# Two attention layers on one TensorE queue: key tiles weighed in pairs behind the former group's sums, the transposed maxima 65 wide, all positions moved

## The reference, cut to what matters

```python
# layer 0: 32 heads of 32; layer 1: 16 heads of 64
dots = einsum('bhnd,bhmd->bhnm', q, k) * scale
attn = softmax(dots, axis=-1)
out = einsum('bhnm,bhmd->bhnd', attn, v) @ w_out + b_out
```

## Time and profile before

| what | us |
|---|---|
| median of 3 runs (lowest to highest) | 3464.93 (3464.24 to 3469.18) |
| the profiled execution, its own time | 3465.76 |
| span of its trace | 3464.0 |
| layer 0, first to last `rows` product (63 groups) | 288.7 to 1479.2 |
| layer 1, the same | 2084.7 to 3199.0 |
| TensorE busy over the span | 3034.1 (88%) |
| DVE, ACT, POOL busy | 2162.0, 1718.8, 1746.4 |

### The profile page before, as it was taken

How to read it: one execution, slowest core, us unless ns; L and a number is a source line. 1 busy time by engine, 2 the same in 40 slices (tenths; PEclk the granted TensorE clock), 3 DMA queues, 4 the chain that set the end, 5 groups by cost and what they waited for, 6 DMA issues and landing times. The chain is left out here.

```text
span 3464.0 us, 46558 instructions
## 1 busy us (share of the span) xinstructions
PE 3034.1 (88%) x16106; PEld 1908.5 (55%) x16106; DVE 2162.0 (62%) x4520; ACT 1718.8 (50%) x3306; POOL 1746.4 (50%) x1540
## 2 busy tenths in 40 slices
PE   7999999999999999988863839999999999999266
PEld 6884455454545555467752835555555555554166
DVE  5567766676676666646665416676666666666642
ACT  5555766666666666656540414444443444443032
POOL 0005878788787878830101824443444445445056
PEclk9999999999999999989985969999999999999578
DMA  2003333333333333300010444443434444433034
GB/s 88 1 19 89 86 85 91 76 82 85 84 85 89 84 84 75 75 25 16 13 41 25 84 95 92 92 98 82 104 86 92 98 95 95 96 86 70 25 69 74
DMA packets 182987, 254.00 MB, mean 73 GB/s; under 512 B 35904, under 2 KB 75584, under 8 KB 182208
## 3 DMA queue, kind: packets, MB, share of 16 engines
q1 hardware_dynamic: 168672, 240.19, 29.4%
q0 software_dynamic: 14080, 10.82, 2.3%
HBM read 33.44 MB, written 16.67 MB: 14 GB/s over the span
## 5 line engine op out<-in xcount | busy, mean ns | idle before, releaser
L1737 POOL TENSOR_TENSOR arena<-arena 128x512 f32<-128x512 f32 x1152 | 1440.7, 1277 | 859.2 <-ACT arena L1119 835.6
L780 PE MATMUL psum<-stack 96*128 96x512 f32 (+4 forms) x4096 | 1330.2, 442 | 60.3 <-DMA stack<-halves 43.4
L1375 DVE TENSOR_REDUCE top<-psum 128x1 f32<-128x512 f32 x1536 | 1001.0, 685 | 401.4 <-PE psum L780 397.4
L1119 ACT ACTIVATE arena<-psum 128x512 f32<-128x512 f32 x1536 | 857.9, 595 | 448.6 <-PE psum L780 441.4
L780 PEld LDWEIGHTS psum<-stack 96*128 96x128 f32 (+4 forms) x4096 | 712.4, 191 | 639.5 <-issue 399.1
L810 PE MATMUL psum<-arena,values 128*32 128x512 f32 (+1 forms) x3072 | 556.5, 617 | 0.1
L1706 POOL TENSOR_SCALAR rstd<-mv 128x4 f32<-128x4 f32 x56 | 12.6, 226 | 579.2 <-DVE mv L1241 577.5
L768 PE MATMUL psum<-xT,wqkv 128*128 128x512 f32 x512 | 268.6, 606 | 6.8 <-DVE arena L1420 3.0
L1407 DVE RECIPROCAL psum<-psum 128x128 f32<-128x128 f32 x256 | 226.4, 926 | 61.0 <-PE psum L840 61.0
L1082 ACT ACTIVATE halves<-psum,bqk 128x512 fp32r<-128x512 f32 x128 | 87.9, 687 | 310.3 <-PE psum L768 310.2
L1327 DVE SCALAR_TENSOR_TENSOR X<-psum,weight,X 128x128 f32<-128x128 f32 x512 | 144.0, 345 | 141.3 <-PE psum L747 141.2
(11 more groups left out here) (154 smaller groups left out, 3054.5 us busy)
## 6 DMA issues: line engine op xcount, KB each, us to landing
stack<-halves SPq DMA_DIRECT2D x768, 128.0 KB, 2.3
stack<-halves SPq DMA_DIRECT2D x384, 256.0 KB, 4.8
tokens<-xn SPq DMA_DIRECT2D x16, 256.0 KB, 2.4
sums<-X SPq DMA_DIRECT2D x16, 256.0 KB, 4.1
wqkv<-in_wg SPq DMA_DIRECT2D x16, 256.0 KB
wqkv<-in_wu SPq DMA_DIRECT2D x16, 256.0 KB
wqkv<-in_wd SPq DMA_DIRECT2D x16, 256.0 KB
wqkv<-in_w_qkv SPq DMA_DIRECT2D x2, 1536.0 KB, 9.9
```

Source lines behind the costliest of these rows:

```text
L780: ins = T_.matmul(bk, st[0:k, side, slot + h, cols], st[0:k, 1 - side, slot + h, :], start=r == 0, stop=r == len(PARTS[l]) - 1)
L1119: S_.activation(prob[l][tile % N_PROB][:, h, :], psum[:, bank[key], :], ACT.Exp, scale=scale).then_inc(released[bank[key]], 1)
L1375: give(V_.reduce_max(top[i][:, j:j + 1], psum[:, bank[key], :], AX.X), key)
L1737: ins = G_.tensor_tensor(to[:, h, :], old[:, h, :], prob[l][tile % N_PROB][:, h, :], ALU.add)
```

## The change

Four things are changed; sizes, arithmetic and results stay.

1. `weigh` is called for two key tiles at a time: key tiles 0 and 1 after the products of key tile 2, key tiles 2 and 3 together in `last`.
2. The sums (`dn`) leave `mix` and become a part of their own, `sums`, placed just before the step of the next group at which key tiles 0 and 1 are weighed.
3. `top` has 65 columns instead of 16, set to zero once at the start, and all 65 are turned.
4. Every position in `WHEN` is set anew for both layers. POOL's steps are cut to the new number of steps of `probs`.

```diff
-    dict(project=(-0.11, 0.67), maxima=(0.97, 1.82), rows=(1.85, 1.85), probs=(2.21, 3.17),
-         last=(3.18, 3.24), mix=(3.51, 4.19), out=(4.24, 5.01), ahead=(-2.20, -0.56),
-         finish=(4.85, 4.85), settle=(5.19, 5.40)),
-    dict(project=(0.12, 0.60), maxima=(1.02, 1.56), rows=(1.78, 1.78), probs=(2.21, 3.17),
-         last=(3.03, 3.30), mix=(3.53, 4.18), out=(4.15, 4.75), ahead=(-2.50, -0.89),
-         route=(4.90, 6.70), keep=(7.45, 7.45)))
+    dict(project=(-0.11, 0.70), maxima=(0.97, 1.84), rows=(1.94, 1.94), probs=(2.25, 3.17), last=(3.25, 3.37),
+         mix=(3.94, 4.55), out=(4.53, 5.01), ahead=(-2.32, -0.75), finish=(4.91, 4.91), settle=(5.57, 5.86)),
+    dict(project=(-0.11, 0.54), maxima=(1.02, 1.60), rows=(1.80, 1.80), probs=(2.32, 3.28), last=(3.18, 3.47),
+         mix=(3.94, 4.52), out=(4.63, 5.17), ahead=(-2.45, -0.80), route=(5.19, 7.18), keep=(8.11, 8.11)))
...
-            queue("probs", (l, n), (heads + 1) * TILES_B - 1, (heads + 1) * TILES_B, n)
-            queue("mix", (l, n), 6, 6, n)
+            queue("probs", (l, n), heads * TILES_B + 1, heads * TILES_B + 1, n)
+            start, end = WHEN[l]["probs"]
+            pair = start + (end - start) * 3 * heads / (heads * TILES_B + 1)
+            stream("sums", (l, n), 1, 1, at + n + 1 + pair - 0.001, at + n + 1 + pair - 0.001)
+            queue("mix", (l, n), 5, 5, n)
...
-        top = [sb(f"top{i}", [P, 16]) for i in range(2)]
+        TOP_WIDTH = P // 2 + 1
+        top = [sb(f"top{i}", [P, TOP_WIDTH]) for i in range(2)]
...
-                T_.matmul(bk[0:n_top, 0:P], top[n % 2][:, 0:n_top], ident, is_transpose=True).then_inc(done, 1)
+                T_.matmul(bk[0:TOP_WIDTH, 0:P], top[n % 2][:, :], ident, is_transpose=True).then_inc(done, 1)
...
-                    if kt:
-                        weigh(l, n, kt - 1)
+                    if kt == 2:
+                        weigh(l, n, 0)
+                        weigh(l, n, 1)
                         yield
...
-            def last_tile(l, n):
-                weigh(l, n, TILES_B - 1)
+            def last_tiles(l, n):
+                weigh(l, n, 2)
+                weigh(l, n, 3)
                 yield
                 yield
...
-            def mix(l, n):
+            def sums_of(l, n):
                 width, i = WIDTH[l], n % 2
                 pe.wait_ge(*tile_summed(l, n, TILES_B - 1))
...
+            for t in top:
+                tick(V_.memset(t[:, :], 0.0), constants_set)
```

More of the change, by code:

```diff
@@ L181, in __init__ @@
                      project=self.project, maxima=self.maxima, rows=self.rows, probs=self.probabilities,
-                     last=self.last, mix=self.mix, out=self.out, finish=self.finish, settle=self.settle, ahead=self.ahead, fold=self.fold, experts1=self.experts1)
+                     last=self.last, sums=self.sums, mix=self.mix, out=self.out, finish=self.finish, settle=self.settle, ahead=self.ahead, fold=self.fold, experts1=self.experts1)
         play(order, parts)
@@ L261, in probabilities @@
                 yield
-            if kt == 1:
+            if kt == 2:
                 self.mixed.take(("o", l, n))
-            if kt:
                 yield
@@ L270, in last, with sums @@
         yield
+    def sums(self, l, n):
+        self.other.take(("dn", l, n))
+        yield
     def mix(self, l, n):
         dn, turned, back = ("dn", l, n), ("turned", l, n), ("back", l, n)
-        self.other.take(dn)
-        yield
         if l == 0:
@@ L843, in mix @@
                 yield
+            def mix(l, n):
                 if l:
                     return
-                columns = [inverse[l][i][:, t * P:(t + 1) * P] for t in range(TILES_B)]
+                columns = [inverse[l][n % 2][:, t * P:(t + 1) * P] for t in range(TILES_B)]
                 yield
@@ L953, in _ @@
             play(order, dict(prepare0=prepare0, route=route, ahead=ahead, compute0=compute0, project=project,
-                             maxima=maxima, rows=rows_of_maxima, probs=probabilities, last=last_tile, mix=mix,
+                             maxima=maxima, rows=rows_of_maxima, probs=probabilities, last=last_tiles, sums=sums_of, mix=mix,
                              out=project_out, fold=fold, experts1=experts1))
@@ L1211, in _ @@
             play(order, dict(load0=load0, prepare0=prepare0, route=route, ahead=ahead, compute0=compute0,
-                             project=project, rows=rows_of_maxima, probs=probabilities, last=last_tile, mix=mix,
+                             project=project, rows=rows_of_maxima, probs=probabilities, last=last_tiles, mix=mix,
                              settle=settle, experts1=experts1))
@@ L1724, in probabilities @@
                     tile = n * TILES_B + kt
-                    for h in range(heads):
+                    for _ in range(heads - 1):
                         yield
```

## The result

The changed kernel takes 3320.21 us (median of 4 runs, 3318.87 to 3321.8), the one before 3466.84 us on the same chip (4 runs): ratio 0.9577, 95% interval 0.9561 to 0.9594. It is faster by 4.2%, 146.6 us. Forecast were 3351 us and a range of 3300 to 3412.

What follows compares the result with a forecast made beforehand. TensorE, busy nearly throughout both attention stages, was taken as the bound. Terms 58 + 35 + 28 + 12 - 19 = 114 us off 3465.8 gave 3351.8, with the runs' median 0.8 lower, 3351 us; range 3300 to 3412.

Steps and rivals of the forecast that it cites:

- The price of a visit, 0.32 us: TensorE's cost per stretch cut into column tiles between whole-array work: way out 0.10, way in 0.09, join inside 0.13 us.
- the prediction's other estimate, 0.11 us: Round trip into column tiles and back on TensorE, from a documented drain of some 128 cycles; visits' term then some 35 us.
- The visits' terms, 58 and 35 us: Gain in layers 0 and 1 from three and two fewer column-tile stretches a group, after the wider maxima's loss.
- The maxima 65 wide: Turning `top` with 65 columns loses 0.05 us a group in layer 0 and 0.09 in layer 1; removes no switch.
- Bunching, 19 us lost: Blocks of sums and two key tiles leave DVE dry 0.8 us a group; 0.15 us lost, 128 times.
- POOL's lateness, 12 us: Layer 0: TensorE's waits for POOL before the sums vanish, slack growing from 0.5 to 4.8 us; 12 us gained.
- The copies, 28 us: Layer 1: earlier k makes DMA copies into `stack` 2 us early, gaining 28 of 30.3 us of TensorE waits.
- A sign of being wrong: Wrong if L780 or loads wait over 0.3 us a group for DVE/ACT, L840 for POOL, or `probs` for maxima's rows.
- the first one: Rival: new order also lifts small stalls in both layers, 38 us more and no bunching loss, some 3295 us; chance 0.12.
- dry banks: Rival: product banks run dry, the whole 0.8 us a group is paid, 102 instead of 19 us, 3434 us; chance 0.11.
- a POOL late in front of the block: Rival "slower": POOL late for layer 0's sums holds everything behind on TensorE, 224 us, so 3575 us; chance 0.05.
- the visits were what was saved: Opposing rival: way in and out lost in waits anyway, only 0.13 us per join stays, 3402 us; chance 0.06.

Runs made afterwards that it cites:

- Run 4: Changed kernel with layer 0's sums 0.04 of a group earlier, q's projection between them and the two key tiles, three visits a group instead of two: 3334.76 us, ratio 0.9622.
- run 5: Changed kernel with only the key tile pairs undone, sums still in front of key tile 1, new positions kept, four visits a group: 3386.67 us, ratio 0.9773.
- run 3: Changed kernel with only the 16 or 8 used columns of `top` turned instead of 65: 3311.61 us, ratio 0.9558.
- run 9: Changed kernel with all four key tiles weighed in `last` behind the former group's sums, `mix` and the rest later, one visit a group: 3610.5 us, ratio 1.0425.
- run 7: Changed kernel with layer 1's `project` at its old late place and its `mix` at 4.02 to 4.60, so v gets the other bank: 3481.34 us, ratio 1.0032.
- run 8: Changed kernel with SP also waiting for v's read before the copies into `stack` in layer 1, nothing else: 3478.71 us in a single execution.
- run 1: Kernel before with the changed kernel's `WHEN` positions alone; key tiles singly, sums at the head of `mix`, `top` narrow: 3552.58 us, ratio 1.0252.
- run 2: Changed kernel with the old positions of `project`, `maxima`, `rows`, `probs` and `ahead`, `last` and `mix` as early as possible: 3695.91 us, ratio 1.0665.
- run 6: Changed kernel with only layer 1's `project` back at its old later place, 0.12 to 0.60: 3538.36 us, ratio 1.0214.

## Why the prediction held, point by point

- **The price of a visit, 0.32 us, was right.** Run 4 shows 0.30 in layer 0, run 5 0.28 (inside group, 17.21 - 16.65, halved) to 0.33; the prediction's other estimate, 0.11 us, is a third of that. The visits' terms, 58 and 35 us, stand: inside groups of layer 0 fell by 0.85 to 0.9 us as forecast.
- **The maxima 65 wide: right**, 0.04 to 0.05 us lost a group in layer 0 (run 3). In layer 1 the lost cover is in the forecast's 0.55 us, and narrow or wide makes no difference there.
- **Bunching, 19 us lost, was mis-sized.** It is near nothing at blocks of 2.7 us: splitting a block (run 4) gave nothing back. A block two key tiles longer went with 1.6 us more a group in layer 0 (run 9), of which its own share is open.
- **POOL's lateness, 12 us, was too small**, and one wait was left out. The group of layer 0 that holds a batch's turn of `xn`, and the one behind it, took 19.36 and 18.92 us before; after, 17.29 and 16.65. These are 2.1 and 2.3 us, where an inside group gained 0.9. The kernel before shows why:

```profile
814.60 1.59 PE L780 MATMUL psum<-stack 96*128 96x512 f32 x4
817.00 1.06 PE L840 MATMUL psum<-arena,ones 128*32 128x512 f32 x8 [0.80 <-POOL arena L1737]
...
826.15 0.63 PE L685 MATMUL psum<-cst,arena 128*128 128x128 f32 x4 [0.97 <-DVE halves L1354]
```

  The four products before the first started at 814.60, so the sums were due at about 815.7 and came 1.3 us late; the bracket says 0.80, since it counts from the modelled end of the former product. The second I had read as 6.7 us in all and left out of the sum. Together they are about 2.6 us beyond the visits in each of seven batches, 18 us. Over layer 0 all waits of TensorE that the profile lists fell from 31.2 to 11.2 us, by 20, where 12 less 9.5 for bunching were forecast: most of what layer 0 gained above forecast. Some 5 us more come from the clock: a mean below 0.97 in five groups before and in two after.
- **The copies, 28 us: right in kind** (33.3 of 34.3 us are gone, and the slack is near what was worked out: runs 7 and 8), but a batch's first groups paid part of it back: k's projection waits for `route`'s block 2.4 us a batch, and q's 0.8 us for `ml`, the low half of the maxima's rows. These new waits are 22.4 us, and 8.6 us of old ones in the same groups went. 35 + 33.3 - 13.8 = 54 us of the 59.5 are so accounted for. That layer 1 came so near its forecast of 53 is in part luck: this cost of 13.8 us nearly cancels against the 9.5 us for bunching, which were not paid, and the 5.3 by which the copies gave more. The prediction named what is late next in layer 1 as the transposition of the maxima; it was the bank of q and k. The sums' longer hold on one of two banks was a cost that I did not price.
- **Positions as additive terms: wrong as a way of reckoning.** I gave them 28 and 12 us and nothing if undone. Runs 1 and 2 show 85 us lost by the positions alone and 228 by the structure alone. Inside the changed structure the term does hold: run 5, with as many visits in layer 1 as before, is 27.2 us faster there. The sum came out because the two were changed together.
- **A sign of being wrong came, and the time held.** I had named waits of the score products (L780, now L783) or of their loads for DVE or ACT of more than 0.3 us a group. In layer 0 the weight loads of L783 waited 72.4 us for DVE and 17.5 for ACT, 1.4 us a group. The sign was badly chosen: before it was 1.0 already, and nearly all is hidden, since the products themselves waited 1.9 and 8.8 us.

The rivals: some of the first one's gain came (stalls of layer 0 lifted), dry banks and a POOL late in front of the block did not, and the visits were what was saved.

## What to carry to other kernels

Price a switch of TensorE's shape from start to start of the instructions around it, in both directions, and gather the tiled work into few blocks: here blocks of 2.7 us cost nothing beyond their work, while with one of 4.5 us the whole kernel was slower than before, for several reasons. Where banks are handed out by a list, a step moved by a few hundredths of a group can be handed another bank and another wait: look who gave it back last. Read a part's move in what TensorE passes on the way, not in fractions of a period: 0.17 of a group was 4.3 us here, not 2.7.

## What the runs showed of the hardware beyond that

A wait of TensorE can cost more than its length. The two windows of layer 1 shown in the section on the result have the same wait of 2.25 us; where the mean granted clock is 0.91 the group is 1.55 us longer than where it is 1.00. Six batches have this wait, and in five of them the slower clock stands behind it. The length of the wait alone does not decide it: in run 8 a group with a wait of 2.86 us kept 1.00, and one with 1.90 us fell to 0.91.

In the run with `project` late, a stretch of 10 us around one wait of 2.28 us, then in full the group of the run with the copies late that holds the wait of 3.21 us (windows; the granted clock is the third number from the right):

```profile
2598.00:2608.00 10.00, 7.72 (x26) 6.18 (x25) 4.76 (x8) 3.61 (x7) 0.00 (x0) 0.68 0.71 158
```

```profile
2558.10:2578.24 20.14, 16.93 (x66) 9.82 (x66) 10.81 (x16) 6.92 (x14) 7.50 (x6) 0.92 0.36 80
```

The mean granted clock there is 0.68 and 0.92, so part of the stretch runs at 1.2 instead of 2.4 GHz: the two records of k take 1.91 us where they take 1.02 at the full clock. Over layer 1 the mean is 0.93 in run 6 and 0.96 in runs 7 and 8, against 0.99 in the changed kernel. In run 8 the clock explains most of what the waits leave open: TensorE's waits in layer 1 grew from 27.4 to 149.3 us, by 121.9, and 29 groups instead of 7 have a mean clock below 0.97. An estimate from these, 22 groups at 1.55 us, adds 34 us; together they are 156 of the 161.5.
